# Order of work on ScalarE and VectorE, and the stores of q, k and the combine table, in the second layer of a two-layer transformer kernel

## The reference

```python
qkv = einsum('bld,ed->ble', x, w_qkv)        # q, k, v: 16 heads x 16
q = rmsnorm(q, q_norm_w); k = rmsnorm(k, k_norm_w)
attn = softmax(einsum('bhqd,bhkd->bhqk', q, k) * D ** -0.5)
out = einsum('bhqk,bhkd->bqhd', attn, v) @ w_proj + b_proj
...
combine = top-2 softmax weights of 8 experts, per token
moe = sum over experts of combine[:, e] * (silu(x @ gw) * (x @ uw) @ dw)
ffn = moe + shared expert
```

## Time and profile before

| what | us |
|---|---|
| three runs | 1397.16, 1397.29, 1399.36 |
| median | 1397.29 |
| the profiled execution, its own time | 1398.46 |
| its span, first to last instruction | 1396.7 |
| TensorE busy in the span | 1352.6 |
| VectorE, ScalarE, GpSimd busy | 906.8, 756.2, 727.8 |
| mean granted TensorE clock | 0.996 |

### The profile page before, as it was taken

How to read it: one execution, slowest core, us unless ns; L and a number is a source line. 1 busy time by engine, 2 the same in 40 slices (tenths; PEclk the granted TensorE clock), 3 DMA queues, 4 the chain that set the end, 5 groups by cost and what they waited for, 6 DMA issues and landing times. The chain is left out here.

```text
span 1396.7 us, 25325 instructions
## 1 busy us (share of the span) xinstructions
PE 1352.6 (97%) x8758; PEld 1205.1 (86%) x8758; DVE 906.8 (65%) x1807; ACT 756.2 (54%) x1964; POOL 727.8 (52%) x719
## 2 busy tenths in 40 slices
PE   8999899999999999999999999889999999999998
PEld 7887798999899989998998898768889888888897
DVE  6655566566656665666565665557887778786765
ACT  4553454445544555455545444246666666666664
POOL 1651343445343555344635453447657676766775
PEclk9999999999999999999999999999999999999999
DMA  5995333224422353234324424266555663645662
GB/s 185 318 337 202 84 91 97 84 77 120 113 82 49 103 144 85 62 91 114 97 63 120 118 63 127 95 189 186 162 169 156 197 176 112 205 138 181 177 194 91
DMA packets 105646, 190.51 MB, mean 136 GB/s; under 512 B 20433, under 2 KB 39569, under 8 KB 103217
## 3 DMA queue, kind: packets, MB, share of 16 engines
q1 hardware_dynamic: 105520, 188.91, 45.5%
HBM read 116.41 MB, written 30.47 MB: 105 GB/s over the span
## 5 line engine op out<-in xcount | busy, mean ns | idle before, releaser
L776 POOL TENSOR_TENSOR a_pr<-a_pr,a_ri 128x512 f32<-128x512 f32 x128 | 133.4, 1042 | 299.9 <-DVE a_ri L956 299.9
L833 ACT ACTIVATE a_pr<-a_score,a_nb 128x256 f32<-128x256 f32 x256 | 119.2, 471 | 267.7 <-DVE a_nb L948 267.7
L1374 POOL TENSOR_TENSOR l_pr<-l_pr,l_ri 128x512 f32<-128x512 f32 x128 | 133.3, 1042 | 126.4 <-DVE l_ri L1730 125.2
L1489 ACT ACTIVATE l_pr<-l_score,l_nb 128x256 f32<-128x256 f32 x256 | 119.3, 472 | 100.7 <-DVE l_nb L1699 100.7
L58 PE MATMUL a_job<-s_xs,s_wh 128*128 128x512 f32 x384 | 153.6, 400 | 1.0 <-PEq L222 1.0
L60 PE MATMUL a_job<-s_xs,s_wl 128*128 128x512 f32 x384 | 152.1, 396 | 0.0
L59 PE MATMUL a_job<-s_xs,s_wh 128*128 128x512 f32 x384 | 151.4, 394 | 0.0
L948 DVE TENSOR_REDUCE a_nb<-a_score 128x2 f32<-128x512 f32 x128 | 88.5, 692 | 86.1 <-PE a_score L1027 84.2
L1699 DVE TENSOR_REDUCE l_nb<-l_score 128x2 f32<-128x512 f32 x128 | 87.5, 684 | 32.1 <-PE l_score L1838 31.9
L961 DVE TENSOR_TENSOR a_pt<-a_turn,a_pt 128x512 fp32r<-128x512 f32 x128 | 87.5, 684 | 23.8 <-ACT a_pt L841 23.8
L58 PE MATMUL l_job<-l_xs,s_wl 128*128 128x512 f32 x224 | 90.3, 403 | 5.9 <-DMA s_wl<-wgu_scratch 5.8
(11 more groups left out here) (252 smaller groups left out, 4565.4 us busy)
## 6 DMA issues: line engine op xcount, KB each, us to landing
s_wl<-wgu_scratch SPq DMA_DIRECT2D x56, 512.0 KB, 5.7
a_sk<-a_rotk SPq DMA_DIRECT2D x384, 64.0 KB, 2.0
a_sq<-a_rotq SPq DMA_DIRECT2D x256, 64.0 KB, 2.0
s_xs<-xn_scratch SPq DMA_DIRECT2D x14, 1024.0 KB, 5.6
l_wd<-wd_scratch SPq DMA_DIRECT2D x56, 256.0 KB, 2.9
l_zq<-qs_scratch SPq DMA_DIRECT2D x128, 64.0 KB, 4.3
l_sk<-ks_scratch SPq DMA_DIRECT2D x32, 256.0 KB, 4.7
a_raw<-in_w SPq DMA_DIRECT2D x30, 256.0 KB, 2.9
```

The source lines that it names most:

```text
L776: pool.tensor_tensor(e, e, ri[:, n % 2, :].unsqueeze(2).broadcast_to([P, 2, SEQ]), ALU.mult)\
L833: i = act.activation(pr[:, n % 2, t, :], PS[n % 2][:, t * SEQ:(t + 1) * SEQ], ACT.Exp, bias=nb[:, n % 2, t:t + 1], accum_out=sm[:, n % 2, ...
L1374: pool.tensor_tensor(e, e, ri[:, n % 3, :].unsqueeze(2).broadcast_to([P, 2, SEQ]), ALU.mult)\
L1489: i = act.activation(pr[:, n % 3, t, :], PS[n % NPS][:, t * SEQ:(t + 1) * SEQ], ACT.Exp, bias=nb[:, n % 3, t:t + 1], accum_out=sm[:, n % 3 ...
```

## The change

Five things change, all for layer 1. On ScalarE, the loop `for K in HID_AT[n]: hid_hi(K)` stands ahead of `exps(n + 1)` and not between the first and second items. On VectorE, the low part of head n-2 comes ahead of the row maximum of n+1. The combine table is stored by ScalarE after its copy; SP keeps the wait for the landing. q and k are stored with two DMAs to a half, four to a batch, with the q rows reordered to head, pair, feature, so that each row holds its high and low part side by side; a load of q then reads two runs of 1 KB for a row where it read one of 2 KB. With the new order the sum of squares and the scaling of q read with a stride of 1 where it was 4 (`q = (1, 8)[r]`), and the weights' rows and the norm weights are laid out to match on the host.

```diff
-                def store_combine(s):
-                    wait_free(sp, ("C", s))
-                    if s >= 2:
-                        sp.wait_ge(S["cmul"], ME * (s - 1))
-                    sp.dma_start(ct_dram[s % 2], ct[:, :]).then_inc(ct_stored[s % 2], 16)
+                def wait_combine(s):
                     sp.wait_ge(ct_stored[s % 2], 16 * (s // 2 + 1))
...
                 def store_stack(m, half):
                     wait_free(sp, (f"X{half}", m))
-                    for low in range(2):
-                        sp.dma_start(qs_dram[m % 2, half, :, :, low].rearrange("h d p n -> (h d) p n"), tqk[:, half, 0, low, :].bitcast(F32))                           .then_inc(tqk_out[half], 16)
-                        sp.dma_start(ks_dram[m % 2, half, :, low].rearrange("h d p n -> (d p) h n"), tqk[:, half, 1, low, :].bitcast(F32))                           .then_inc(tqk_out[half], 16)
+                    sp.dma_start(qs_dram[m % 2, half].rearrange("h p d l n -> (h p d) (l n)"),
+                                 tqk[:, half, 0, :, :].rearrange("r l n -> r (l n)").bitcast(F32)).then_inc(tqk_out[half], 16)
+                    sp.dma_start(ks_dram[m % 2, half].rearrange("h l d p n -> (d p) h l n"), tqk[:, half, 1, :, :].bitcast(F32))\
+                      .then_inc(tqk_out[half], 16)
...
-                        own = qs_dram[m % 2, half, h, :, :, j:j + PER_LOAD].rearrange("d c p n -> (d c) (p n)")
+                        own = qs_dram[m % 2, half, h, j:j + PER_LOAD].rearrange("p d c n -> (d c) p n")
                         for base in (64 * h, 64 * h + 32):
-                            sp.dma_start(zq[base:base + 32, h, at, :].bitcast(F32).rearrange("k p n -> k (p n)"), own)                               .then_inc(zq_in[stack_of(i)], 16)
+                            sp.dma_start(zq[base:base + 32, h, at, :].bitcast(F32), own)                               .then_inc(zq_in[stack_of(i)], 16)
...
                         act.activation(ct[:, :], bank[0:E, :], ACT.Copy, scale=0.5).then_inc(free_of(item), 1)
+                        wait_free(act, item)
+                        if m >= 2:
+                            act.wait_ge(S["cmul"], ME * (m - 1))
+                        act.dma_start(ct_dram[m % 2], ct[:, :]).then_inc(ct_stored[m % 2], 16)
...
+                    for K in HID_AT[n]:
+                        hid_hi(K)
                     if 0 <= n + 1 < N:
                         exps(n + 1)
                     for item in first:
                         job_out(item)
-                    for K in HID_AT[n]:
-                        hid_hi(K)
...
                 def sum_squares(m, r):
-                    q = (4, 8)[r]
+                    q = (1, 8)[r]
...
                 def scale_rows(m, r):
-                    q = (4, 8)[r]
+                    q = (1, 8)[r]
...
+                    if 0 <= n - 2 < N:
+                        dve.wait_ge(S["turn_hi"], n - 1)
+                        dve.tensor_tensor(pt[:, n % 2, 1, :], PT[:, :], pt[:, n % 2, 0, :], ALU.subtract).then_inc(S["turn_free"], 1)
                     if 0 <= n + 1 < N:
                         dve.wait_ge(S["score_full"], n + 2)
                         dve.tensor_reduce(nb[:, (n + 1) % 3, :], PS[(n + 1) % NPS][:, :].rearrange("p (t k) -> p t k", t=2), AX.X,
                                           ALU.max, negate=True).then_inc(S["max_ready"], 1)
-                    if 0 <= n - 2 < N:
-                        dve.wait_ge(S["turn_hi"], n - 1)
-                        dve.tensor_tensor(pt[:, n % 2, 1, :], PT[:, :], pt[:, n % 2, 0, :], ALU.subtract).then_inc(S["turn_free"], 1)
```

More of the change, by code:

```diff
@@ L1281, in load_stack @@
                     if p % 4 == 0:
-                        sp.wait_ge(tqk_out[p // 4], 16 * 4 * (m + 1))
+                        sp.wait_ge(tqk_out[p // 4], 16 * 2 * (m + 1))
                     if pair >= NSTK:
@@ L1326, in _ @@
                         stack_until(AT["C", s])
-                        store_combine(s)
+                        wait_combine(s)
                     if K >= 1 and not is_shared(K - 1):
@@ L1458, in job_out @@
                         if m >= 1:
-                            act.wait_ge(tqk_out[half], 16 * 4 * m)
+                            act.wait_ge(tqk_out[half], 16 * 2 * m)
                         act.activation(tqk[:, half, 0, 0, :], bank[:, 0:SEQ], ACT.Copy, scale=sh.nqk[:, 0:1])
@@ L1895, in program @@
     ct = nc.dram_tensor("ct_scratch", [2, E, STEP], F32, kind="Internal").ap()
-    qs = nc.dram_tensor("qs_scratch", [2, 2, 2, D1, 2, 4, SEQ], F32, kind="Internal").ap()
+    qs = nc.dram_tensor("qs_scratch", [2, 2, 2, 4, D1, 2, SEQ], F32, kind="Internal").ap()
     ks = nc.dram_tensor("ks_scratch", [2, 2, 2, 2, D1, 4, SEQ], F32, kind="Internal").ap()
@@ L1922, in head_columns @@
     q, k = w[0:2 * D].reshape(2, 2, 4, 2, D1, D)
-    return np.concatenate([q.transpose(0, 2, 3, 1, 4).reshape(D, D), k.transpose(0, 3, 1, 2, 4).reshape(D, D), w[2 * D:]])
+    return np.concatenate([q.transpose(0, 2, 1, 3, 4).reshape(D, D), k.transpose(0, 3, 1, 2, 4).reshape(D, D), w[2 * D:]])
 def proj_rows(w):
@@ L1988 @@
         "w_qkv": head_columns(i["L1_attn_w_qkv"]).T, "w_proj": proj_rows(i["L1_attn_w_proj"].T),
-        "norm_w": _np.stack([_np.tile(_np.repeat(i[f"L1_attn_{s}_norm_w"], 4), 2) for s in "qk"], axis=1),
+        "norm_w": _np.stack([_np.tile(i[f"L1_attn_{s}_norm_w"], 8) for s in "qk"], axis=1),
         "b_proj": i["L1_attn_b_proj"][None],
```

## The result

The changed kernel takes 1470.58 us in the median of 4 runs (1469.78 to 1471.73), the kernel before 1397.22: ratio 1.052, interval [1.0507, 1.0532], 73.4 us slower. The prediction said slower with 0.87, at 1428 in a range up to 1446: the sign was right, and the size was not: 31 us were forecast and 73.4 measured.

A forecast was written before the change was run, and what follows sets the result against it. The prediction took TensorE as the bound, busy 420.30 of 434.00 us in layer 1's attention slots. From 1398.46 us, +34 (hid_hi) +1 (low part) -4 (stores) -1 (shared tiles) gave 1428.5, stated as 1428, range 1403 to 1446.

The forecast's parts named there:

- The moved hid_hi decides: ScalarE, layer 1 slots: hid_hi's wait for GpSimd's combine now holds up exps and the next scores, for 42 combines.
- Its price, 34 us: Cost of moving hid_hi on ScalarE: 17 for two-slot pairs, 15 for first tiles, 2 for the rest; bounds 0 to 84.
- The ten first tiles of a run: Routed tiles after a longer gap or a shared tile: 1.5 us of delay each, 15 us together.
- The 24 two-slot pairs: Routed tiles two slots apart: loop through combine, hid_hi and exps takes 7.8 us against 7.08, 17 us together.
- The five three-slot gaps and the one of one slot: Routed tiles three slots apart, five times, and one apart, once: 2 us together.
- The low part ahead of the maximum, 1 us: VectorE order: slack hides later exps; waiting for ScalarE's high part costs 1 us in some dozen slots.
- the 0.71 of slack: Time from the end of a slot's exponentials to TensorE's next scores, 0.71 us; only longer delays reach TensorE.
- Shared tiles, -1: hid_hi of the 12 shared tiles waits for VectorE only and fills ScalarE's 0.9 us gap: 0 or 1 us gained.
- The stores, -4 between 0 and -7: Start of layer 1 slots: gu load 4.3 us earlier, TensorE's 5.80 us wait becomes 1.4; gain 4, between 0 and 7.
- The rule that another issuer saves only the issue time: Trainium skill's rule: the combine table's store by ScalarE would be worth 0.54 us; the prediction took 2.3.
- zq loads in 1 KB runs, and the stride of 1: Loads of q covered by early issue, 0 us; sum of squares and scaling 5 us either way, taken as 0.
- Rival 4: Worse, chance 0.05: TensorE's repeated 1 us waits lower the granted clock, 43 us more, about 1470.

The follow-up runs named there:

- wait_combine: Kernel before, with ScalarE's exponentials also waiting for GpSimd's combine, hid_hi itself staying behind them: 1436.27 us, ratio 1.0286.
- hid_combine_ahead: Kernel before, with hid_hi ahead of exps and, on GpSimd, the combine of first-item tiles ahead of normalise: 1427.14 us, ratio 1.0212.
- stores_hid_last: Kernel before, with the new stores and hid_hi moved behind ScalarE's second items: 1384.37 us, ratio 0.9911.
- low_alone: Kernel before, with only the low part moved ahead of the row maximum on VectorE: 1433.08 us, ratio 1.0253.
- wait_copy: Kernel before, with the maximum of n+1 also waiting for ScalarE's high copy of n-2, the low part staying behind it: 1407.39 us, ratio 1.0077.
- low_half_ahead: Kernel before, with the low part cut into two 256-element operations, one ahead of the maximum and one behind: 1417.57 us, ratio 1.014.
- the two idle operations: Two runs of the kernel before, with an idle VectorE operation ahead of each maximum: 224 elements 1436.78 us, 512 elements 1468.54 us.
- stores_hid_shared: Kernel before, with the new stores and hid_hi ahead of exps for the 12 shared tiles alone: 1392.18 us, ratio 0.9966.
- stores_alone: Kernel before, with only the stores changed (combine table issued by ScalarE, four q and k stores a batch, q reordered): 1391.38 us, ratio 0.9953.
- table_by_scalar: Kernel before, with only the combine table's store issued by ScalarE: 1396.42 us in 10 runs, ratio 0.9993.
- hid_alone: Kernel before, with only hid_hi moved ahead of exps on ScalarE: 1449.65 us, ratio 1.0375.
- dummy_short: Kernel before, with an idle 224-element VectorE operation ahead of each maximum, the low part behind it: 1436.78 us, ratio 1.0279.

## Why the prediction was right in sign and wrong in size

1. **The moved hid_hi decides, by a wait for the combine in front of the exponentials.** Right for the largest part, and shown: wait_combine has 38.9 of 52.5 us with the wait alone, hid_combine_ahead gives 22 back by taking normalise out, stores_hid_last gains by moving it the other way.
2. **Its price, 34 us.** Mis-sized. The profile shows which terms held. I summed the lengths of the slots from score to score, before and after, by the groups of the plan. The ten first tiles of a run: 15 us forecast, 14.7 found. The 24 two-slot pairs: 7.8 us each forecast; 13 of them take 7.6 to 8.0, as the pair above, but the others take up to 9.9: 31.1 us against 17. I priced the loop as an empty one; in many of the long ones the plan has X items or merges, which also need VectorE, ScalarE and GpSimd. That they are the reason was not tested. The five three-slot gaps and the one of one slot: 10.1 against 2. That is 56 us in place of 34 in the changed kernel, where the low part has its share; by itself hid_hi measures 52.5, and on top of the low part and the stores 41.6.
3. **The low part ahead of the maximum, 1 us.** This is the step that failed. It said that the turn starts 0.6 earlier, exps end 0.6 later, and "against the 0.71 of slack the scores then start where they did". That can be true of one slot by itself. But the reciprocal and the second items stand behind those exponentials in VectorE's queue, and the next low part and maximum behind them, so the next slot can begin late with the slack already used. I had put the low part's 0.6 in the loop of hid_hi and had left it out of the loop that every slot has. low_alone measures 35.9 in place of 1, with the scores waiting 14.7 us for exponentials and VectorE idle 42.4 us ahead of the reciprocal where it was 14.9. Of this, the wait for ScalarE's late copy, which I had at 1, is 10 us when it is added by itself (wait_copy). low_half_ahead (20.3) and the two idle operations (39.6 and 71) agree that time ahead of the maximum in VectorE's queue costs, but theirs is lost at the turns and not at the scores.
4. **Shared tiles, -1.** stores_hid_shared shows no difference, and could not show one of 1 us.
5. **The stores, -4 between 0 and -7.** Right by themselves: -5.8. The sum of my steps, 2.0 for the four stores and 2.3 for the table, fits the load, issued at 920.32 in stores_alone and not at 924.94. In the changed kernel it was taken back at once: the fifth pair of score matmuls starts at 944.3 before, at 940.0 in stores_alone and at 944.1 in the changed kernel. After the load TensorE waited there for exps(0), behind hid_hi(4), as the step says:

```profile
927.32 0.47 PE L58 MATMUL l_job<-l_xs,s_wl 128*128 128x512 f32 x1 [2.82 <-DMA s_wl<-wgu_scratch]
...
932.36 0.79 PE L1839 MATMUL l_score<-l_sk,l_zq 128*128 128x256 f32 x2 [1.66 <-ACT l_pr L1490]
```

6. **The rule that another issuer saves only the issue time** (the Trainium skill, "Trainium Kernel Development and Optimization", Key Constraints). I put it aside because SP also stood still for the landing. In the row of table_by_scalar the wait is 2.2 us shorter, more than the issue; in the time, by itself, it is nothing that can be told.
7. **zq loads in 1 KB runs, and the stride of 1.** Right at 0. The load lands in 4.5 us (4.3 in the earlier trace rows), and no score waits for it in the changed kernel. The sum of squares over q got shorter, first before, then after:

```profile
l_zq<-qs_scratch SPq DMA_DIRECT2D x128, 64.0 KB, 4.5
```

```profile
L1625 DVE TENSOR_REDUCE l_ss<-l_sqr x16: 1048/1104/1172, 899.2 to 1283.1; 128x32 f32<-128x512 f32 x16
```

```profile
L1626 DVE TENSOR_REDUCE l_ss<-l_sqr x16: 673/890/1185, 897.9 to 1342.8; 128x32 f32<-128x512 f32 x16
```

8. **The rivals.** None of them was it. The time lies beyond the forecast case. Rival 4 had named 1470, and 1470.58 was measured, but that is luck: its cause was the clock, which stayed at 0.99 over the slots, worth some 5 of 506 us by my estimate. The missing case was one I had no rival for: both orders cost, each by its own loop.

Of the signs that the prediction named, four came: the scores' wait for l_pr (42.9 us in 54 pieces), the longer wait ahead of l_hid, the turns' shorter wait, and TensorE's share of 89%. ScalarE's wait ahead of l_pr did not shrink but grew: hid_hi shortens it (64.2 in hid_alone), and the low part lengthens it (177.9 in low_alone). The first gap was 2.82 us and not 1.4.

Stated as one sum: 52.5 (hid_hi) + 35.9 (low part) - 5.8 (stores) - 9.2 (overlap of the parts) = 73.4.

## What to carry to other kernels

A wait moved ahead of the work that closes a recurring loop can be paid once in each round, as the wait for the combine was here (38.9 us for some 42 tiles); before moving it, walk the loop for two rounds, not for one, since a delay that one slot's slack absorbs is still in the queue of the next. Work that lies in the shadow of another engine's step (here the low part beside the exponentials) was free only there; the same work one place earlier is in the chain. A test that costs one line is to add the wait without the work, or the work without the wait, and to see which of the two the time follows; but look at where the waits then stand, since added work can lose its time in another place than moved work, as the idle operations did here. And an engine busy for 97% is no proof that the others have slack: here VectorE's chain was as tight as TensorE.

## What the runs showed that I had not expected

- With TensorE busy 97% of the stage, time put ahead of the maximum on VectorE, which is busy 76% of it, still came through: 39.6 us for 65 more of work and 71 for 105, and 35.9 for 127 x 0.60 = 76 us that were only moved.
- An operation from SBUF to SBUF on VectorE (512 elements, float32) took from 664 to 1795 ns, median 822, mean 935, while the low part, which reads PSUM and SBUF, takes 0.68. The short one ranged to 1493. GpSimd's normalise got longer in the run with the long one, 1218 ns in the mean against 1042. I have not tested what stretches either.
- A store of a half of q, 256 KB, was issued in 0.32 us when each row was one run of 2 KB; two of 128 KB took 0.60 each before. The timeline of the SP queue in the run with the stores alone:

```profile
915.46 0.32 SPq L1269 DMA_DIRECT2D qs_scratch<-l_tqk  x1
915.82 0.63 SPq L1271 DMA_DIRECT2D ks_scratch<-l_tqk  x1
...
920.32 0.43 SPq L1248 DMA_DIRECT2D s_wl<-wgu_scratch  x1
```

- The granted clock of 925 to 940 us was 1.00 behind the idle TensorE of 2.02 us in stores_alone, 0.89 behind the 3.56 us of table_by_scalar, 0.77 behind 5.80 us, and 0.66 in the changed kernel behind 2.82 and 1.66 us. The length of the idle time ahead does not order them: in dummy_short it was 5.12 us, and the clock 0.89.
